# Attention probabilities that stay in PSUM and are transposed by DMA, in a graph attention kernel

## The reference

```
# block 0: two layers on h = x
a    = softmax(h h^T / sqrt(384)); delta = a * adj; attn = delta / (sum(delta) + 1e-10)
ctx  = (attn*upper) @ (h Wl^T + bl) + diag(attn) * (h Ws^T + bs) + (attn*lower) @ (h Wr^T + br)
h    = relu(layernorm(ctx) * ln_w + ln_b)
# x = layernorm(x + h)
# block 1: 12 heads of 32
s    = q k^T / sqrt(32) + beta * adj, and -9e15 where adj is 0
out  = softmax(s) @ v
# x = layernorm(x + out)
```

## Time and profile before

| | |
|---|---|
| median of 3 runs | 1965.3 us (1962.09 to 1965.7) |
| profiled execution | 1962.81 us, span 1960.9 us |
| PE busy | 1866.0 us, 95% of the span |
| PE weight loads busy | 1802.3 us, 92% |
| DVE busy | 1617.7 us, 82% |
| ACT busy | 1259.4 us, 64% |
| POOL busy | 669.3 us, 34% |
| mean granted clock of TensorE | 0.975 |

### The profile page before, as it was taken

One profiled execution on the slowest core, in us unless ns is written; L12 is line 12 of the kernel. 1 busy time (PEld: TensorE's weight loads), 2 busy tenths in 40 slices (PEclk: granted clock), 3 DMA queues, 4 the chain that ended last, 5 costly groups with the idle time before them and its releaser, 6 DMA issues.

```text
span 1960.9 us, 43643 instructions
## 1 busy us (share of the span) xinstructions
PE 1866.0 (95%) x14656; PEld 1802.3 (92%) x14656; DVE 1617.7 (82%) x5318; ACT 1259.4 (64%) x3612; POOL 669.3 (34%) x775
## 2 busy tenths in 40 slices
PE   4899999999999999999999999999999999999975
PEld 4799999999999999999999999999999999999964
DVE  4568888888888988888888888898888888888875
ACT  3356667666666766666766666676666676666653
POOL 0223432333333334343233333333434323333331
PEclk9899999999999999999999999999999999999975
DMA  4033322233332223332223333222333222333310
GB/s 148 27 79 80 88 67 59 69 90 82 84 80 64 61 80 90 82 84 66 63 65 90 82 84 81 62 61 79 90 82 84 68 62 65 90 82 84 82 43 23
DMA packets 144548, 147.18 MB, mean 75 GB/s; under 512 B 17596, under 2 KB 144328, under 8 KB 144328
## 3 DMA queue, kind: packets, MB, share of 16 engines
q1 hardware_dynamic: 133424, 131.20, 25.3%
q10 hardware_dynamic: 10904, 13.20, 1.9%
HBM read 56.25 MB, written 12.58 MB: 35 GB/s over the span
## 4 chain that ended last, share of the span: by engine, by line
PE 83%; DVE 12%; issue 2%; ACT 2%; POOL 0%; DMA 0%; ACTq 0%; POOLq 0%; DVEq 0%
PE bank_w L367 43%; PE bank_m L367 10%; PE bank_p L510 8%; PE bank_u L367 7%; PE bank_o L367 5%; PE bank_s L367 5%; DVE normed L802 2%; DVE masked L858 2%; DVE pT_lo L864 2%; PE bank_t L384 1%; PE bank_u L449 1%; DVE stats_y L819 1%; PE bank_t L395 1%; DVE normed L816 1%; PE bank_t L374 1%
## 5 line engine op out<-in xcount | busy, mean ns | idle before, releaser
L657 ACT ACTIVATE prob<-masked,hmin 128x256 f32<-128x256 f32 x768 | 383.7, 503 | 67.5 <-DVE hmin L858 60.9
L858 DVE CUSTOM_DVE_ANT_0 masked<-bank_s,bias_adj 128x256 f32<-128x256 f32 x768 | 292.3, 418 | 63.6 <-PE bank_s L367 61.0
L664 ACT ACTIVATE pT_hi<-bank_p 128x512 f16<-128x512 f32 x384 | 227.8, 593 | 89.1 <-PE bank_p L510 77.6
L864 DVE TENSOR_TENSOR pT_lo<-bank_p,pT_hi 128x512 f16<-128x512 f32 x384 | 262.2, 683 | 13.4 <-ACT pT_hi L664 11.5
L510 PE MATMUL bank_p<-ident,prob 128*128 128x128 f32 x1536 | 243.4, 282 | 12.8 <-DVE pT_lo L864 8.9
L604 ACT ACTIVATE hlrh<-bank_w 128x384 fp32r<-128x384 f32 x256 | 120.9, 484 | 159.4 <-PE bank_w L367 159.4
L367 PE MATMUL bank_w<-w_graph0h,hT_ach 128*128 128x384 f32 x576 | 203.5, 353 | 7.5 <-DVE w_graph0l L716 7.3
L950 POOL TENSOR_SCALAR v_rest<-adj_in 128x512 f32<-128x512 f32 x32 | 62.1, 1940 | 430.3 <-issue 428.5
L510 PEld LDWEIGHTS bank_p<-ident,prob 128*128 128x128 f32 x1536 | 178.9, 145 | 25.9 <-issue 19.0
L367 PE MATMUL bank_w<-w_graph1h,hT_bh 128*128 128x384 f32 x576 | 200.5, 348 | 0.0
L367 PE MATMUL bank_w<-w_graph0l,hT_ach 128*128 128x384 f32 x576 | 195.4, 339 | 0.0
(11 more groups left out here) (197 smaller groups left out, 5782.0 us busy)
## 6 DMA issues: line engine op xcount, KB each, us to landing
x_in<-in_x SPq DMA_DIRECT2D x64, 384.0 KB, 3.2
adj_in<-in_adj SPq DMA_DIRECT2D x96, 256.0 KB, 3.3
q_st<-qk_hi SPq DMA_DIRECT2D x256, 96.0 KB, 2.2
k_st<-qk_hi SPq DMA_DIRECT2D x256, 96.0 KB, 2.2
q_st<-qk_lo SPq DMA_DIRECT2D x128, 96.0 KB, 2.2
k_st<-qk_lo SPq DMA_DIRECT2D x128, 96.0 KB, 2.2
out<-result ACTq DMA_DIRECT2D x32, 384.0 KB, 2.5
prob<-in_L_gnn_Wl SPq DMA_DIRECT2D x2, 192.0 KB, 4.0
```

The costliest lines, as they stand in the source:

```text
L657: nc.scalar.activation(prob[:, h % 2, i, :], masked[:, i, :], ACT.Exp, bias=hmin[:, i, h:h + 1], scale=-1.0, accum_out=hsum[:, i, HEADS[h] ...
L664: nc.scalar.activation(pT_hi[:, h % 2, :, :].rearrange("p j i -> p (j i)"), bank_p[:, :], ACT.Copy).then_inc(s_pt_hi, 1)
L858: ve.tensor_tensor_reduce(masked[:, i, :], bank_s[:, i * S:(i + 1) * S], bias_adj[:, i, :], -SCALE, BIG, ALU.add, ALU.min, hmin[:, i, h:h ...
L864: ve.tensor_tensor(pT_lo[:, h % 2, :, :].rearrange("p j i -> p (j i)"), bank_p[:, :], pT_hi[:, h % 2, :, :].rearrange("p j i -> p (j i)"), ...
```

## The change

The change has five parts.

1. Two banks, `bank_s[0]` and `bank_s[1]`, take the place of `bank_s` and `bank_p`. The mask, the exponential and the split of a head all work in its bank, in place; `masked`, `prob` and the row sum are gone. ACT's copy and DVE's rest write float16 `halves` in SBUF, not transposed.
2. The step `weights` leaves PE. SP issues one transposing DMA for each head, from `halves` [128, 1024] float16 to `pT` [128, 8, 128], two buffers of each. It waits for DVE's rest and for attend k-2. `scores` on PE waits for the rest of head k-2, and ACT's copy for transfer k-2.
3. `v_parts` gets a 33rd column of ones, so that `bank_o` holds the row sums. Each `attend` on DVE takes a small reciprocal.
4. The graph softmax is exponentiated in place in `bank_u`, as is one copy in `turn_h`; the three scalings of `h_apply`, `b_out` and `c_apply` go to ACT, each with a small product `shift` on DVE.
5. The orders of PE, ACT, DVE and POOL are written anew, and SP gets one.

The bias rows are also held in six rows of one tile, with six small selecting matrices.

```diff
+VC = 33
 ORDER = {
     "pe": """
+        attend.4-1 a_proj.4-1 scores.8-1 a_proj.5-1 turn_y.0-1 attend.5-1 scores.9-1 turn_y.1-1 a_mix.0-1
+        attend.6-1 turn_y.2-1 attend.7-1 scores.10-1 a_mix.1-1 q.0 q.1 q.2 scores.11-1 k.0 attend.8-1
+        attend.9-1 turn_h.0 k.1 k.2 turn_h.1 v.0 turn_h.2 attend.10-1 v.1 turn_x.0 attend.11-1 b_scores.0
+        turn_x.1 scores.0 b_proj.0 scores.1 b_proj.1 b_proj.2 b_proj.3 b_turn.0 scores.2 turn_x.2 b_proj.4
+        scores.3 b_proj.5 a_scores.0 scores.4 b_mix.0 attend.0 scores.5 b_mix.1 attend.1 a_proj.0 a_proj.1
+        a_turn.0 attend.2 scores.6 attend.3 a_proj.2 scores.7 a_proj.3""",
...
+    "sp": """
+        weights.5-1 k_stack.3-1 q_stack.3-1 weights.6-1 a_x.0 weights.7-1 c_adj.0 weights.8-1 weights.9-1
+        weights.10-1 q_stack.0 weights.11-1 k_stack.0 k_stack.1 b_adj.0 weights.0 q_stack.1 k_stack.2 a_adj.0
+        weights.1 b_x.0 weights.2 q_stack.2 weights.3 weights.4""",
...
+            def weights(t, k):
+
+                s = t - 2
+                sp.wait_ge(s_pt_lo, NH * s + k + 1)
+                wait(sp, s_pv, NH * s + k - 1)
+                sp.dma_start_transpose(pT[:, k % 2, :, :], halves[:, k % 2, :, :, :].rearrange("p i a s -> p (i a s)")
+                                       ).then_inc(s_pt[k % 2], 16)
...
-                wait(pe, s_msk, NT * (NH * s + k))
-                for i in range(NT):
-                    last = mm(bank_s[:, i * S:(i + 1) * S], q_st[0:SLOTS * HD, h, i * P:(i + 1) * P],
+                wait(pe, s_pt_lo, NH * s + k - 1)
+                for i in range(NT):
+                    last = mm(bank_s[k % 2][:, i * S:(i + 1) * S], q_st[0:SLOTS * HD, h, i * P:(i + 1) * P],
                               k_st[0:SLOTS * HD, h, :], True, True)
...
-            def weights(t, h):
-                s = t - 2
-                pe.wait_ge(s_prob, NT * (NH * s + h + 1))
-                wait(pe, s_pt_lo, NH * s + h)
-                for j in range(NT):
-                    for i in range(NT):
-                        last = nc.tensor.transpose(bank_p[:, j * S + i * P:j * S + (i + 1) * P],
-                                                   prob[:, h % 2, i, j * P:(j + 1) * P], ident[:, :])
-                last.then_inc(s_pt, 1)
...
-                pe.wait_ge(s_pt_lo, NH * s + k + 1)
+                pe.wait_ge(s_pt[b], 16 * (NH // 2 * s + k // 2 + 1))
...
-                        mm(bank_o[:, at:at + VP * HD], pT_hi[:, b, j, i * P:(i + 1) * P], vp, j == 0, False)
-                        last = mm(bank_o[:, at:at + 2 * HD], pT_lo[:, b, j, i * P:(i + 1) * P], vp[:, 0:2 * HD],
+                        mm(bank_o[:, at:at + VP * VC], pT[:, b, 4 * i + j, :], vp, j == 0, False)
+                        last = mm(bank_o[:, at:at + 2 * VC], pT[:, b, 4 * i + 2 + j, :], vp[:, 0:2 * VC],
...
             def graph_exp(n):
                 act.wait_ge(s_ub, n + 1)
-                wait(act, s_at, n)
-                for i in range(NT):
-                    nc.scalar.activation(expu[:, i, :], bank_u[:, i * S:(i + 1) * S], ACT.Exp, bias=ubias[:, i:i + 1],
+                for i in range(NT):
+                    nc.scalar.activation(bank_u[:, i * S:(i + 1) * S], bank_u[:, i * S:(i + 1) * S], ACT.Exp, bias=ubias[:, i:i + 1],
...
+            def scaled(dst, src, k, index, done):
+
+                act.wait_ge(s_shift[k], index + 1)
+                for i in range(NT):
+                    nc.scalar.activation(dst[:, i, :], src[:, i, :], ACT.Identity, bias=shift[k][:, i:i + 1],
+                                         scale=rstd[k][:, i:i + 1]).then_inc(done, 1)
...
+            def scores(t, k):
                 s = t - 2
+                bank = bank_s[k % 2]
+                act.wait_ge(s_msk, NT * (NH * s + k + 1))
+                for i in range(NT):
+                    nc.scalar.activation(bank[:, i * S:(i + 1) * S], bank[:, i * S:(i + 1) * S], ACT.Exp,
+                                         bias=hmin[:, i, k:k + 1], scale=-1.0).then_inc(s_prob, 1)
+
+            def weights(t, k):
+
+                s = t - 2
+                act.wait_ge(s_prob, NT * (NH * s + k + 1))
+                wait(act, s_pt[k % 2], 16 * (NH // 2 * s + k // 2))
+                nc.scalar.activation(halves[:, k % 2, :, 0, :], bank_s[k % 2][:, :].rearrange("p (i s) -> p i s", i=NT),
+                                     ACT.Copy).then_inc(s_pt_hi, 1)
...
+                for i in range(NT):
+                    ve.tensor_tensor_reduce(bank_s[k % 2][:, i * S:(i + 1) * S], bank_s[k % 2][:, i * S:(i + 1) * S], bias_adj[:, i, :],
+                                            -SCALE, BIG, ALU.add, ALU.min, hmin[:, i, k:k + 1]).then_inc(s_msk, 1)
+
+            def weights(t, k):
+                dve.wait_ge(s_pt_hi, NH * (t - 2) + k + 1)
+                ve.tensor_tensor(halves[:, k % 2, :, 1, :], bank_s[k % 2][:, :].rearrange("p (i s) -> p i s", i=NT), halves[:, k % 2, :, 0, :], ALU.subtract
+                                 ).then_inc(s_pt_lo, 1)
...
+                ve.reciprocal(hinv[:, :, a:b + 1:b - a], parts[:, :, :, HD, 0])
+                ve.tensor_reduce(att[:, :, a:b + 1:b - a, :], parts[:, :, :, 0:HD, :], AX.X, ALU.add).then_inc(s_att, 1)
```

More of the change, by code:

```diff
@@ L46 @@
     "pe": """
[L47 to L51, removed]
@@ L61 @@
-    "dve": """
[L62 to L69, removed]
@@ new lines @@
+    "dve": """
+        scores.8-1 weights.7-1 a_proj.4-1 a_proj.5-1 turn_y.0-1 scores.9-1 attend.5-1 turn_y.1-1 weights.8-1
+        a_mix.0-1 scores.10-1 turn_y.2-1 weights.9-1 a_mix.1-1 h_norm.0 q.0 h_apply.0 q.1 attend.7-1
+        scores.11-1 q.2 weights.10-1 k.0 attend.9-1 turn_h.0 k.1 weights.11-1 turn_h.1 k.2 turn_h.2
+        attend.11-1 v.0 turn_x.0 scores.0 v.1 b_scores.0 scores.1 b_proj.0 turn_x.1 weights.0 b_proj.1
+        c_stat.0 b_mask.0 c_stat.1 scores.2 weights.1 c_norm.0 turn_x.2 b_turn.0 scores.3 weights.2 b_proj.4
+        c_apply.0 b_proj.5 weights.3 a_scores.0 scores.4 b_mix.0 a_mask.0 b_mix.1 b_norm.0 weights.4 b_apply.0
+        attend.1 scores.5 a_proj.0 scores.6 attend.3 weights.5 a_proj.1 scores.7 b_resid.0 b_resid.1 b_norm2.0
+        weights.6 b_out.0 a_turn.0""",
@@ L85 @@
 STAGE_D = ("c_sum", "c_stat", "c_norm", "c_apply", "c_store")
-STAGE_C = ("q", "k", "v", "scores", "weights", "attend")
+STAGE_C = ("q", "k", "v", "scores", "weights", "attend", "c_adj", "q_stack", "k_stack")
 def schedule(engine, t, batches):
@@ L278, in pipeline @@
                 todo = []
-                if order == "pool" and t < 3:
+                if order == "pool" and t == 2:
                     todo.append(("split", t, t))
@@ L351, in load, with body_and_weights @@
                                  ).then_inc(s_stage[n], 16)
-            def body_and_weights(t):
-                body(t)
-                if t == 0:
-                    load(0)
-                    load(1)
-            for t in range(NB + 2):
-                body_and_weights(t)
+            steps = {
+                "c_adj": c_adj, "a_x": a_x, "b_adj": b_adj, "b_x": b_x, "a_adj": a_adj, "weights": weights,
+                "q_stack": lambda t, r: stack(t, 0, r), "k_stack": lambda t, r: stack(t, 1, r),
+            }
+            def body_and_weights(t, todo):
+                run(steps, todo)
+                for n in {0: (0, 1)}.get(t, ()):
+                    load(n)
+            pipeline(sp, "sp", body_and_weights)
             sp.wait_ge(s_out, 16 * NB)
@@ new lines, in attend @@
+            def attend(t, k):
+                s, a, b = t - 2, HEADS[k - 1], HEADS[k]
+                if k == 1:
+                    wait(dve, s_out, 16 * s)
+                dve.wait_ge(s_pv, NH * s + k + 1)
+                parts = bank_o[:, 0:NT * 2 * VP * VC].rearrange("p (i h a d) -> p i h d a", i=NT, h=2, a=VP)
+                ve.reciprocal(hinv[:, :, a:b + 1:b - a], parts[:, :, :, HD, 0])
+                ve.tensor_reduce(att[:, :, a:b + 1:b - a, :], parts[:, :, :, 0:HD, :], AX.X, ALU.add).then_inc(s_att, 1)
@@ L894, in c_apply @@
                 refine("c", t - 3)
[L895 to L897 removed]
+                shifted("c")
             def a_mask(t, _k):
```

281 lines of the change are left out of this document (126 added, 155 removed).

## The result

The changed kernel takes 1934.63 us (median of 4 runs, 1929.75 to 1941.28), the kernel before 1964.51 in the same session. The ratio is 0.9852 [0.9821, 0.9883]: 1.5% faster, where 1854 us (5.6%) was forecast. It lies inside the range given, 81 us above the forecast.

The account below looks back on a forecast made before the run. The prediction took PE's own work as the bound. A turn was 52.1 + 0.25 + 1.0 + 0.35 = 53.7 us, 3.57 less than 57.27; over 31 turns 111 us less, giving 1854 us, range 1795 to 1945.

Parts of the forecast that it names:

- fill and drain: Before and after the steady turns: transposes lost and a transfer gained taken to change nothing, 10 us either way.
- 5.5 us transfer: Rival, transposing DMA: at 5.5 us attends 3, 7, 10 and 11 wait, turn 58.0 us, total 1988, slower; chance 0.07.
- a held SP: Rival, SP's queue: issuing a transpose costs 4.8 us, turn 74.7 us, total 2505 us; chance 0.07.
- The bound of 5.5: Upper bound of one head's transfer: 1024 short pieces at 57.5 ns each, 3.7 us, plus 1.85 fixed.
- What the denser queues cost: Engine orders: besides today's 0.25 us a turn, 0.35 added for DVE at 90% and exponentials waiting for both mask halves.
- 1.0 for transfers: PE's attends: with a 3.7 us transfer, 1.0 us a turn of waiting, all at attend.7.
- The prediction's own sign: Steady window: forecast right if PE is busy at 97% or more of 53 to 54 us turns.
- 0.25 us not explained: Kernel before: PE's priced list of 57.0 us against a measured turn of 57.27, the remainder left unexplained.
- Without slack on DVE every late item shows on PE: DVE's order: the reason given for adding 0.35 us a turn, with DVE busy 90%.
- attend.7: Head 7's attend on PE: 2.75 us after attend.5 ends, against a 3.7 us transfer, so it waits 0.95 us.
- DVE becomes the bound: Rival: DVE has 47.6 to 50.0 us of work, keeps 6 idle; turn 54.5 to 56, total 1880 to 1925; chance 0.19 (1875 to 1945).
- The transfer is hidden: Rival: at 2.8 us and no crowding nothing waits, turn 52.1 to 52.4 us, total 1810; chance 0.22.

Follow-up runs that it names:

- PE relief: Kernel before with one transpose of four for each head, all four only in the very first: 1919.54 us, ratio 0.9784.
- 2.3 us more for DVE: Changed kernel with three buffers and the scalings of `h_apply`, `b_out` and `c_apply` back on DVE: 1965.22 us, ratio 1.0011 against the kernel before.
- half the rest: DVE's rest made of half its columns, the other half keeping old values: kernel before 1948.18 us, changed kernel 1907.00, changed kernel with three buffers 1874.89.
- the constant tile: Changed kernel, attend reading a constant tile without waiting for transfers, nor SP for attend; ACT's copy still waits: 1890.27 us, 44 us under the changed kernel.

## Why the prediction was wrong

**What was right.** The kernel before had PE as its bound: 83% of its last chain. PE's list lost what was said: the twelve weights steps, 4.7 us in the starts of one turn before (5.2 with a wait at the step behind one of them), 4.92 forecast. Full clock in the steady stretch held. The fill and drain came to nothing, as taken: 1934.6 - 31x57.1 = 164 us, before 1964.5 - 31x58.0 = 167. DVE lost 1.9 us a turn, 1.65 forecast; ACT stayed far from its bound (38.9, at most 42.7 was said). The transfer took 3.1 us in the median and 3.4 in the mean against 3.7 taken, and SP was held 1.25 us against 1.0. So the rivals of a 5.5 us transfer and of a held SP fell, though single transfers do take 4.8 to 5.5. The bound of 5.5 had the number of pieces right, 1024 for a head, and their price wrong: 0.452x16x3.12/1056 = 21 ns a packet (an estimate from the row above), not 57.5. The Trainium skill's 1309 ns a block by DMA (VectorE: DVE Perf Modes, "The three transpose paths") is not paid one after the other here: eight blocks land in 3.1 us.

**The step that failed** is "What the denser queues cost", for which "I add 0.35". The forecast turn is 52.1 us of PE, 1.0 for transfers and 0.6 for all other waits, 53.7. Measured, it is 52.1 + 1.4 + 3.6 = 57.1, the 1.4 being what the kernel whose attend waits for no transfer is faster by. Of the 3.4 us in which the two differ, 3.0 are the other waits, and 0.4 attend's waits for transfers. The prediction's own sign, PE busy at 97% of turns of 53 to 54 us, was 94.5% of 57.1. 0.75 of those 3.0 was there before the change: the turn was 58.0 us, not 57.27, so "0.25 us not explained" was 1.0.

*DVE has no room.* It is busy 48.0 us, in a fixed order, on single banks. The prediction named this ("Without slack on DVE every late item shows on PE") and then gave it 0.35 us, a tenth of the 3.6 that all the other waits come to. The runs: PE relief of some 3.4 us passes 1.3 with no transfer in the kernel; it passes more once DVE is relieved too (80 us for 43 + 15); 2.3 us more for DVE costs 2.1 a turn. The old turn hid most of it: there half the rest gave 15 us, in the changed kernel 28.

*ACT's copy waits for the transfer of two heads earlier.* The change has that wait, and the description of it says so, but the prediction priced only SP's wait for attend: "What matters is thus the distance in PE's list from the end of attend k-2 to the start of attend k". The copy's wait of 3.6 us a turn on ACT delays DVE's rest and all behind it, and PE meets it at b_mix.1. A third buffer removes it, for 29 us. It is part of the 3.6. A third buffer and half the rest add up (29 and 28 singly, 60 together), so it costs time beside DVE's load.

*attend.7* was rightly named as a place where PE waits for transfers, 0.95 us forecast. The wait there is 0.7 us (mean over 13 turns of its start less its price). But attend.11, which was given none, waits 0.8 us in the mean, mostly 1.7 to 1.8 us in every third turn, and attend.2 0.4, in every third turn too: their transfers then take 4.7 to 5.5 us. That the forecast of 1.0 for all transfers comes near the measured 1.4 is in part luck. The reason given for attend.7 was only half right, too. It is not the distance from attend.5, since a third buffer leaves the wait as it is; head 7's own copy and rest come late, and its transfer takes 3.9 us.

**The rivals.** "DVE becomes the bound" (54.5 to 56 us a turn, 1880 to 1925) had the mechanism but was priced by the idle time that DVE would keep, 6 us at most; it kept 9.1 (57.1 - 48.0). The measured 1934.6 lies beyond that rival's 1925. "Against it: its waits are on PE and ACT, and shrink when it is late itself" is where it went wrong: DVE idled 8.1 us a turn before and idles 9.1 now, and the wait of its rest for ACT's copy alone went from 11.5 us in all to 29.6. "The transfer is hidden" fell with the 44 us.

**What stays open.** How the 3.6 us divide among the single banks `bank_m` and `bank_t`, the order, and the copies that wait for a buffer is not settled: three buffers and the constant tile overlap in what they remove and were not run together. Nor was it tested what the late transfers of every third turn cost. The shortest turns take 55.5 us, 1.6 less than the mean, but the stores of the kernel with the constant tile are unevenly spaced as well (54.6 to 57.5 us). Nor was an order planned afresh for three buffers, or SP's (in the three-buffer kernel head 6's transfer stands behind six stack DMAs, issued 0.86 us after its rest was done).

## What to carry to other kernels

Work taken from the bounding engine comes back as time only as far as the next engine can follow. Before pricing such a change, ask of the second engine what its idle time is made of, and check the claim cheaply by leaving out some of the first engine's work in the old kernel: that one run (43 us for about 105) would have shown that most of such a relief does not pass. When a step becomes an asynchronous transfer, price every wait on its buffers, on the side that fills them as well as on the side that reads them, and look at it turn by turn: the median of 3.1 us hid that every third one of some heads takes 4.8. And count turns by instructions in a steady window, not by all the outputs, whose distance takes in the shorter last turns.

## What the runs showed of the hardware

- A transposing DMA of 128 x 1024 float16 from SBUF to SBUF lands 3.1 us after its issue (3.0 to 5.5, mean 3.4) and holds SP's queue 1.25 us (up to 2.5), about two stack DMAs (0.6 each). It moves 1056 packets for 0.26 MB, 1024 of them of 256 B, at an estimated 21 ns each: the whole execution has 423100 packets under 512 B, the kernel before 17596. In 1434 to 1454 us the queue has 6000 packets for 2.31 MB, where the earlier trace rows has 2960 for 2.62 MB. The DMA share of the steady stretch rose from 0.28 to 0.62.
- Some transfers land 1.7 us later, at 4.8 us, in every third turn, in the changed kernel and with three buffers alike (heads 5 and 11). Before one such landing, in 731.65 to 732.65 us, the queue's 29 packets take 58.9% of the 16 engines, an estimated 0.32 us each (0.589x16/29), and move 16 GB/s, against 128 over the span. The cause is open.
- In place in PSUM, the mask takes 446 ns (418 with SBUF as its destination) and the exponential 450 (503 from SBUF to SBUF with a row sum). The longer mask does not show in DVE's sum: its work fell by 1.9 us a turn where 1.65 was forecast with no price for PSUM.
- A reciprocal of 128 x 4 from PSUM is 178 ns long, but the sum behind it starts 0.09 to 0.10 us after it.
